# A 12-stage transformer kernel: first weights of seven stages requested one stage earlier, causal spreading on three engines

## The reference

```
for ffn, attn in ((L0_ffn, L0_attn), (L1_ffn, L1_attn), (L2_ffn, L2_attn), (L3_ffn, L3_attn)):
    x = x + 0.5 * ffn(LN(x))
    x = x + attn(LN(x))
    x = x + 0.5 * ffn(LN(x))
```

```
probs = softmax(x @ Wr + br); gate = probs * keep(probs)          # L3_ffn
h = relu(einsum('bth,ehf->betf', x, W1) + b1)
y = einsum('betf,efh->beth', h, W2) + b2
return einsum('bte,beth->bth', gate, y)
```

```
q, k = rotary(x @ Wq + bq), rotary(x @ Wk + bk)
att = q @ k.T + rel_bias_table[bucket]      # causal softmax, then @ v, then Wp
```

## Time and profile before

| | |
|---|---|
| three runs | 3776.59, 3785.52, 3787.69 us; median 3785.52 |
| profiled execution | 3787.19 us; its span 3785.4 us, mean granted clock of PE 0.921 |
| busy, whole span | PE 3336.2 us (88%), DVE 2643.7 (70%), ACT 1901.5 (50%), POOL 1041.7 (28%) |
| l1_ffn | 668.4 to 1085 and 1886 to 2300 |
| l2_ffn, l2_attn, l2_ffn | 2300 to 2433.7, to 2503.8, to 2636.3 |
| l3_ffn, l3_attn, l3_ffn | 2636.3 to 2899.4, to 3533.9, to 3785 |
| busy in l3_attn (634.4 us) | PE 557.9, DVE 439.2, ACT 384.7, POOL 139.2 |

### The profile page before, as it was taken

How to read it: one execution, slowest core, us unless ns; L and a number is a source line. 1 busy time by engine, 2 the same in 40 slices (tenths; PEclk the granted TensorE clock), 3 DMA queues, 4 the chain that set the end, 5 groups by cost and what they waited for, 6 DMA issues and landing times. The chain is left out here.

```text
span 3785.4 us, 55832 instructions
## 1 busy us (share of the span) xinstructions
PE 3336.2 (88%) x21901; PEld 1709.0 (45%) x21909; DVE 2643.7 (70%) x5660; ACT 1901.5 (50%) x3422; POOL 1041.7 (28%) x832
## 2 busy tenths in 40 slices
PE   4678875899979999999889988888998898899899
PEld 3212234565633333333356665656775322332577
DVE  8787778777749999999377773454434777784433
ACT  2232222677756777777567772223223366766321
POOL 0344561867621000000096660001202111311100
PEclk9779977999988999999999998979999699999899
DMA  0000000311100000000021110001100000000100
GB/s 21 9 0 1 0 1 1 87 27 35 27 5 1 1 1 1 1 1 1 17 75 32 28 24 24 6 24 37 56 1 28 1 1 1 1 1 1 46 1 12
DMA packets 49631, 60.16 MB, mean 16 GB/s; under 512 B 9364, under 2 KB 34328, under 8 KB 49240
## 3 DMA queue, kind: packets, MB, share of 16 engines
q1 hardware_dynamic: 49368, 56.59, 5.4%
HBM read 39.22 MB, written 1.10 MB: 11 GB/s over the span
## 5 line engine op out<-in xcount | busy, mean ns | idle before, releaser
L142 PE MATMUL ps<-AR 128*128 128x128 f32 (+8 forms) x16848 | 2137.9, 434 | 152.1 <-DVE AR L114 36.7
L131 ACT ACTIVATE AR<-ps 128x512 f32<-128x512 f32 (+6 forms) x1808 | 1279.9, 748 | 1130.9 <-PE ps L142 856.2
L142 PEld LDWEIGHTS ps<-AR 128*128 128x128 f32 (+5 forms) x16848 | 1029.6, 152 | 1288.0 <-DVE AR L125 393.1
L125 DVE TENSOR_REDUCE AR<-ps 128x1 f32<-128x512 f32 (+1 forms) x1424 | 935.8, 708 | 117.1 <-PE ps L142 116.5
L114 POOL TENSOR_TENSOR AR<-AR 128x512 f32<-128x512 f32 (+5 forms) x486 | 622.0, 1293 | 793.9 <-ACT AR L131 553.0
L131 ACT ACTIVATE AR<-ps,AR 128x128 f32<-128x128 f32 (+2 forms) x700 | 355.8, 526 | 320.2 <-PE ps L142 292.5
L114 POOL TENSOR_TENSOR rs<-rs,halves 128x4 f32<-128x4 f32 x64 | 67.9, 1062 | 1495.1 <-DVE rs L118 1494.3
L142 PE MATMUL ps<-XT,AR 128*128 128x512 f32 x896 | 439.1, 626 | 20.3 <-DMA AR<-in_L3f_w 8.4
L114 DVE TENSOR_TENSOR AR<-ps,AR 128x512 f32<-128x512 f32 (+3 forms) x626 | 299.1, 527 | 131.1 <-PE ps L142 90.4
L122 DVE SCALAR_TENSOR_TENSOR X<-ps,AR,X 128x128 f32<-128x128 f32 x512 | 143.6, 343 | 339.9 <-PE ps L142 339.7
L150 PE MATMUL ps<-C,AR 128*128 128x128 f32 (+1 forms) x1593 | 249.2, 292 | 109.1 <-DVE AR L114 46.9
(11 more groups left out here) (82 smaller groups left out, 1766.8 us busy)
## 6 DMA issues: line engine op xcount, KB each, us to landing
AR<-AR SPq DMA_DIRECT2D x124, 128.0 KB, 2.3
AR<-in_c_rot SPq DMA_DIRECT2D x64, 128.0 KB, 2.2
AR<-in_L3f_w SPq DMA_DIRECT2D x32, 256.0 KB, 5.8
AR<-in_L2f_w SPq DMA_DIRECT2D x32, 128.0 KB, 2.9
AR<-scr_bias SPq DMA_DIRECT2D x32, 128.0 KB, 3.1
WR<-in_c_rot SPq DMA_DIRECT2D x4, 512.0 KB, 5.9
WR<-in_L_ffn_wqkv SPq DMA_DIRECT2D x2, 768.0 KB, 5.4
AR<-in_L_ffn_wqkv SPq DMA_DIRECT2D x2, 768.0 KB
```

What stands on the lines that cost most here:

```text
L125: return self.do(lambda e: e.tensor_reduce(o, a, AXX, op, negate=neg, apply_absolute_value=mag), *w)
L131: return self.do(lambda e: e.activation(o, a, f, bias=bias, scale=scale, accum_out=acc), *w)
L142: last = e.matmul(o, l, r, start=a, stop=z, skip_group_check=True)
```

## The change

After the code of a stage and ahead of the barrier, a new function `fetch_ahead` asks for the next stage's first weights, into the part of `WR` that neither stage uses: for both l1_ffn `QS` of both layers and `WQ` of the first; for l2_ffn and l3_ffn (two each) expert 0's first matrix and the router; for l2_attn all weights. That makes seven starts of stages. In l3_attn, whose rotation tables lie in that part of `WR`, the load waits for the last rotary instruction (`g.t_turn`). The remaining loads stay where they are. In the causal attention the spreading is divided anew: ACT makes RAW and HI (now without mask), POOL makes QK by a two-operation scaling, DVE makes MQK = HI * mask + RAW in one three-operand instruction. The spreading of l1_attn stays.

```diff
+        g.t_turn = None
+        g.d_two = [DmaSem(sem("d_ah%d" % i)) for i in range(2)]
+        g.d_ah = g.d_two[0]
...
             stage(g)
+            if not g.last:
+                fetch_ahead(g, stages[k + 1])
             barrier(g)
...
+def fetch_ahead(g, stage):
+
+    S, I, wr = g.S, g.I, g.wr
+    g.d_ah = g.d_two[(g.d_ah is g.d_two[0]) * 1]
+    if stage is l1_ffn:
+        wr.at = 2152
+        g.wq0, g.qs0 = wr.f32(1536), [wr.f32(4, 64) for _ in range(2)]
+        for l in range(2):
+            g.t_ahead = g.d_ah.load(S, g.qs0[l], I["h_qs"][l])
+        g.t_ahead = g.d_ah.load(S, g.wq0, I["L1_ffn_wqkv"][0])
+    elif stage in (l2_ffn, l3_ffn):
+        wr.at, n, pre = (1714, 256, "L2f_") if stage is l2_ffn else (3664, 512, "L3f_")
+        g.w10, g.wrt = wr.f32(n), wr.f32(8)
+        g.d_ah.load(S, g.w10, I[pre + "w1"][:, 0, :], g.t_turn)
+        g.t_ahead = g.d_ah.load(S, g.wrt, I[pre + "wr"])
+    elif stage is l2_attn:
+        wr.at = 2152
+        g.l2w = wr.f32(4, 128), wr.f32(2), wr.f32(3, 128), wr.f32(NT, 2)
+        for k, n in enumerate(("wq", "wk", "wv", "wo")):
+            g.d_ah.load(S, g.l2w[0][:, k, :], I["L2a_" + n])
+        g.d_ah.load(S, g.l2w[1], I["L2a_bq"])
+        g.d_ah.load(S, g.l2w[2], I["L2a_bb"])
+        g.t_ahead = g.d_ah.load(S, g.l2w[3], I["c_sc"])
...
-        wts.append(dict(WQ=m.f32(1536), WO=m.f32(4, 128), W1=m.f32(682), W2=m.f32(3, 128), B1=m.f32(6), LG=m.f32(2),
-                        B2=m.f32(128), QS=m.f32(4, 64)))
-    for l, w in enumerate(wts):
-        tqs = g.d_h.load(S, w["QS"], I["h_qs"][l])
-    twq = g.d_r.load(S, wts[0]["WQ"], I["L1_ffn_wqkv"][0])
+        wts.append(dict(WQ=ar.f32(1536) if l else g.wq0, WO=m.f32(4, 128), W1=m.f32(682), W2=m.f32(3, 128), B1=m.f32(6), LG=m.f32(2),
+                        B2=m.f32(128), QS=g.qs0[l]))
+    assert g.wr.at <= 1714
+    twq = tqs = g.t_ahead
     tqs = [V.ts(w["QS"][:, 0:2, :], w["QS"][:, 0:2, :], 8.0, None, ALU.mult, None, tqs) for w in wts][-1]
...
         traw = g.free[b] = A.act(RAW[:, x, :], g.bank[b], ACT.Copy, t, hif[x])
-        thi = A.act(HI[:, x, :], RAW[:, x, :], ACT.Copy, traw, tw, scale=MK[:, 1 + k:2 + k])
+        thi = A.act(HI[:, x, :], RAW[:, x, :], ACT.Copy, traw, tw, scale=1.0 if causal else MK[:, 1 + k:2 + k])
         tqk = None
-        if not k:
+        if causal:
+            tqk = G.ts(QK[:, k, s, cols], RAW[:, x, :], MK[:, 0:1], MK[:, 3:4] if k else None, ALU.mult,
+                       ALU.add if k else None, traw, tw, skf[s])
+        elif not k:
             tqk = A.act(QK[:, 0, s, cols], RAW[:, x, :], ACT.Copy, traw, tw, skf[s], scale=MK[:, 0:1])
-        elif causal:
-            tqk = A.act(QK[:, 1, s, cols], RAW[:, x, :], ACT.Identity, traw, tw, skf[s], scale=MK[:, 0:1], bias=MK[:, 3:4])
         return gr, c, k, x, traw, thi, tqk
 
     def spread_low(gr, c, k, x, traw, thi, tqk):
         s, cols = gr % slots, slice(512 * c, 512 * c + 512)
-        t = G.tt(MQK[:, k, s, cols], HI[:, x, :], RAW[:, x, :], ALU.add, thi)
+        if causal:
+            t = V.stt(MQK[:, k, s, cols], HI[:, x, :], MK[:, 1 + k:2 + k], RAW[:, x, :], ALU.mult, ALU.add, thi, tw)
+        else:
+            t = G.tt(MQK[:, k, s, cols], HI[:, x, :], RAW[:, x, :], ALU.add, thi)
         if tqk is None:
             tqk = V.ts(QK[:, 1, s, cols], RAW[:, x, :], MK[:, 0:1], MK[:, 3:4], ALU.mult, ALU.add, traw, tw, skf[s])
         hif[x] = tsp[gr, c, k] = [t, tqk]
...
+    g.t_turn = list(trc.values()) if causal else None
...
-    W = ar.f32(4, 128)
-    bq = ar.f32(2)
-    bb = ar.f32(3, 128)
-    sc = ar.f32(NT, 2)
-    for k, n in enumerate(("wq", "wk", "wv", "wo")):
-        g.d_w.load(S, W[:, k, :], I["L2a_" + n])
-    g.d_w.load(S, bq, I["L2a_bq"])
-    g.d_w.load(S, bb, I["L2a_bb"])
-    tw = g.d_w.load(S, sc, I["c_sc"])
+    W, bq, bb, sc = g.l2w
+    tw = g.t_ahead
...
-    W1 = ar.f32(8, nf * 128)
+    W1 = ar.f32(7, nf * 128)
+    W1 = [g.w10] + [W1[:, e, :] for e in range(7)]
     W2 = ar.f32(8, nf, 128)
-    WR = ar.f32(8)
+    WR = g.wrt
+    tah = g.t_ahead
     BR = ar.f32(8)
     LT = ar.f32(2, 8, 8)
-    g.d_w.load(S, WR, I[pre + "wr"])
     g.d_w.load(S, BR, I[pre + "br"]) if not top2 else None
     tw = g.d_w.load(S, LT, I["c_lt"])
...
         d = (g.d_ms + g.d_ps)[e]
-        d.load(S, W1[:, e, :], I[pre + "w1"][:, e, :])
+        if e:
+            d.load(S, W1[e], I[pre + "w1"][:, e, :])
         tex.append(d.load(S, W2[:, e, :, :], I[pre + "w2"][:, e, :, :]))
...
-            t = P.mm([(g.bank[b], W1[:, e, 128 * m1:128 * m1 + 128], g.XT[:, 512 * c:512 * c + 512], True, True)],
-                     g.free[b], tex[e], *w)
+            t = P.mm([(g.bank[b], W1[e][:, 128 * m1:128 * m1 + 128], g.XT[:, 512 * c:512 * c + 512], True, True)],
+                     g.free[b], tex[e] if e else tah, *w)
...
-                    tT, tw, g.free[6])
+                    tT, tah, g.free[6])
...
-    t = g.P.mm(parts, th, g.free[b])
+    t = g.P.mm(parts, th, g.free[b], tex[e])
```

More of the change, by code:

```diff
@@ L1906, in moe @@
             if len(todo) > 1:
-                moe_down(g, todo.pop(0), HT, W2, L2, nf, hf, tg, txs)
+                moe_down(g, todo.pop(0), HT, W2, L2, nf, hf, tg, txs, tex)
             if bias_steps and 3 <= e < 7:
@@ L1913, in moe, with moe_down @@
                 gate_add(*gates.pop(0))
-    moe_down(g, todo.pop(0), HT, W2, L2, nf, hf, tg, txs)
-def moe_down(g, what, HT, W2, L2, nf, hf, tg, txs):
+    moe_down(g, todo.pop(0), HT, W2, L2, nf, hf, tg, txs, tex)
+def moe_down(g, what, HT, W2, L2, nf, hf, tg, txs, tex):
     e, c, th = what
```

## The result

The changed kernel took 3761.09 us (median of 4 runs, 3758.14 to 3763.0) against 3786.61 before: a ratio of 0.9941, 95% interval 0.9925 to 0.9958. 3766 was forecast, from 3756 to 3780. The profiled execution has a span of 3761.1 us.

What follows compares the result with a forecast made beforehand. The prediction saw PE held by weight DMAs at seven stage starts, and a PE, DVE and ACT ring in l3_attn. Fetches 17.0, clock 2, head 1.0 and diagonal 1.0 made 21 us: 3787.19 to 3766, range 3756 to 3780.

Steps and rivals of the forecast that it cites:

- The gaps: PE's waits for weights at the starts of l2_ffn, l2_attn and second l3_ffn close whole: 9.2 us.
- PE's clock: At the stage starts, PE's clock may rise earlier without the gaps: 2 us taken, between 8 gained and 4 lost.
- l1_ffn: Both l1_ffn starts: PE's first product comes 3.3 us earlier each, 6.6 together; ends 2.8 and 8.4.
- Next behind it are the rotation tables: In l1_ffn the next wait is for rotation tables, moved up by three issues (1.4 us) and 768 KB less ahead.
- Rival 1: In l1_ffn the rotation tables replace the weights as the wait: gain 2.8 instead of 6.6, total 3772; chance 0.14.
- The first l3_ffn: The weight gap closes, but PE then waits for the bias table behind the logits: gain 1.2 us, ends 0 and 4.2.
- the two issues that left: First l3_ffn: the bias table's issue moves up by two issues, 0.46 us each, that left the stage's list.
- In the loop: l3_attn's looped spreads: the 0.69 us multiply-add fits DVE's 1.34 us idle time, so it is free.
- the 1.0 us: Head of l3_attn: PE's first product of maxima comes earlier, 1.0 us taken, ends -2 and 2.0.
- delays these by about 1.3 us a chunk: Head of l3_attn: two multiply-adds on DVE between chunks delay the next chunk's rotary products by about 1.3 us.
- Near the diagonal: Last group's steps of l3_attn: ACT is on the chain and loses a pass at some three places; 1.0 of 2.0 us taken.
- Rivals 3 and 4: Looped l3_attn spreads: multiply-add on the path, 3785 (chance 0.17); or it also waits for POOL's pass, 3812 (chance 0.06).

Runs made afterwards that it cites:

- e8: e3 with the l1_ffn rotation tables of tiles 1 to 3 asked for ahead of the stage's other weights; 3757.83 us, ratio 0.9924.
- e1: The changed kernel with the causal spreading put back as before, all fetches kept; 3759.59 us, ratio 0.9935.
- e11: The changed kernel run once more, unaltered; 3762.97 us, ratio 0.9939.
- e3: The changed kernel with the three bias-table loads of the first l3_ffn also asked for a stage earlier; 3757.39 us, ratio 0.993.
- e5: e3 with the causal spreading put back as before; 3760.69 us, ratio 0.9931.
- e6: e3 with DVE's multiply-add done twice in each of the 32 causal spreads; 3771.17 us, ratio 0.9966.
- e10: e8 with the MQK sums of the first two groups of heads put back from DVE to POOL; 3762.84 us, ratio 0.9941.
- e7: e3 with QK made by ACT instead of POOL, and made twice; 3771.52 us, ratio 0.9964.

## Why the prediction was right, point by point

**The gaps.** In l2_ffn, l2_attn and the second l3_ffn the step held to the letter: no DMA releases PE, and in l2_attn and the second l3_ffn 1.2 and 3.9 us came for 1.2 and 4.2 (the l2_ffn stand under PE's clock). The second matrices, masks and biases that stayed in the stage cost nothing.

**l1_ffn.** "Next behind it are the rotation tables" was right, but the term was taken from PE's first product (forecast 672.05, measured 671.76), and what the stage hangs on next is POOL, which is released by the tables: at 674.94 instead of 679.11, 4.2 us earlier, and 3.0 in the second stage (8.0 instead of 11.0 us into it). PE is 4.3 and 3.3 us ahead after 60 products. So the tables moved up by two to three times the 1.4 us that three issues give, more than the issues alone; that the rest is the 768 KB no longer ahead of them, which the prediction named and did not price, no run shows by itself. The stages ended with 6.7 and 3.8, together 10.5, above the upper end of 8.4. e8 shows that little more hangs on the tables: another 4 us earlier on POOL were worth 0.5 us at the first stage's end. Where the first one gains its last 2 us is not settled; they come late in the stage, at places where its clock differs. Rival 1 had the right next wait and the wrong sign: the tables came so much earlier that they gave more than PE's gap.

**The first l3_ffn.** A new gap behind the logits, ended by the bias table, came as said; it is 4.91 us (3.5 in e1 and e11) instead of about 3. The table's issue moved up by 1.1 us, as "the two issues that left" say. In e1 and e11 the table landed 1.2 us earlier than before (16.8 us into the stage instead of 18.1), which is the forecast; in the profile of the result it landed at 18.2, because two of the last matrices were slower (landed at 16.5 and 17.7 us, in e1 at 14.7 and 16.1), and the term came to nothing there. The gain of 1.2 was 1.4 in the mean of three profiles and -0.4 in the one of the result. The price of leaving the table behind is e3's 5.5 us against that profile, 3.4 in the means.

**PE's clock.** 2 us were taken. Beyond their gaps the two l2_ffn gained 1.0 and 1.3, the second l3_ffn lost 0.3, so 2 of the 23 us. That this is the 2 of the forecast is in part luck, since the two profiles without fetches differ by as much in one stage. The prediction weighed an early rise against a fall in the logits, and took the middle; the runs show both in one start. In the second l3_ffn the first products gained 1.44 us and the logits and the products behind them lost 1.65. In l1_ffn the first row of products was 1.4 us shorter in the first stage and 1.0 longer in the second (8.22 against 7.19).

**Spreading.** In the loop the step was right as worked out. In the head the 1.0 us came at PE and ended at DVE, because the last multiply-add stands ahead of the first maxima; "delays these by about 1.3 us a chunk" was put into the sum at the wrong place. Near the diagonal 1.0 was taken, and this term was too small: the products of 380 to 420 us gained 3.4 us against the kernel before and more against e1 and e5, in every profile with the new spreading, part of it by the clock, which no longer fell there. In the changed kernel's profile the lower clock between 125 and 200 us took 3.8 us back (79.2 against 75.4), which the prediction did not have. Whether the new spreading makes this fall likelier is open: it stood in six of the nine profiles with the new spreading, in none of the three with the old one.

**Rivals 3 and 4.** The multiply-add is not on the path in a typical looped spread (0.68 us of idle time are left; a second one would not fit everywhere, e6). Where it meets POOL, they do lose time. In the changed kernel's head (DVE, then POOL):

```profile
2902.02 2.02 DVE L122 SCALAR_TENSOR_TENSOR AR<-AR 128x512 bf16<-128x512 bf16 x2 [0.61 <-ACT AR L131]
```

```profile
2902.80 1.71 POOL L119 TENSOR_SCALAR AR<-AR 128x512 f32<-128x512 f32 x1
```

Two passes of 0.75 and one of POOL, which takes 0.76 where DVE has no such pass (e10), fill 2902.02 to 2904.51: 2.5 us for 2.26 of work, as if one after the other. That agrees with what the Trainium skill, "SBUF — State Buffer", section "Who interferes with whom", says of such a pair. In the loop they seldom meet, as the prediction had it: all 24 multiply-adds took 0.74 or 0.75 us there, and one of POOL's 24 scalings took longer than alone. In the head they meet often, which it did not have: three of the eight multiply-adds and six of the eight scalings took longer. In all the multiply-adds took 25.1 us, 1.1 more than 32 x 0.75, and the scalings 40.2, 3.1 more than 16 x 0.76 + 16 x 1.56. With no scaling on POOL (e7) all 32 multiply-adds took 0.74 to 0.75 us, and with no multiply-add in the head (e10) POOL's eight scalings there took 0.76 and 1.56 to 1.58. The prediction read 0.28 us a pass from a mean of 0.97; of those 96 passes in the kernel before, 67 took 0.68 or 0.69 us and 29 took 1.15 to 2.00, all of these beside a POOL pass. The price of a meeting is thus about a whole pass, not a fraction of one, and what kept it small in the sum is how seldom they meet.

The total is 4.5 us more than forecast (25.5 against 21): 4 more from fetches, 2 less from spreading, and the rest lies within what the lengths of the two attention stages differ from run to run (l1_attn, whose code is unchanged, took 2.5 us less in the profile after). That it comes out this near is in part luck: l1_ffn gave 3.9 us more than was taken, and the spreading's gain near the diagonal was given back by the clock.

## What to carry to other kernels

A stage's first wait is worth only what lies between it and the next wait on any engine: follow each load of the list to its reader, since a small table behind the big weights (here 2 KB behind 3.75 MB) decides as much as the weights. When a pass is moved to another engine, look at both ends of the stretch, and at more than the typical step: idle time of 1.34 us there takes a pass of 0.74, but a second pass cost 6 us in the head of the stage. And where executions of one kernel differ by more than the effect, compare stages at like clock, over several profiles, before a cause is given.

## What the runs showed of the hardware that was not expected

- Stages with identical instructions took 798 or 805 us, once 801 (l1_attn), by the clock granted in their first 100 us.
- A load of 2 KB issued behind 15 or 16 of 256 KB each landed only after the last of them: 7.6 us after its issue in the changed kernel, 6.2 to 6.6 in five other profiles.
- POOL's scaling of 128x512 by a per-partition scalar takes 0.76 us alone, with a second per-partition operand 1.56, more than its sum of two tensors (1.16).
